# Gated attention with two heads a step on different rows of the array

## The chip, the cores and the metric

One program on one core of a Trainium2 chip. The metric is the device time of one execution in microseconds; the kernel before was run three times, median 1127.7 us (1127.27 to 1127.97).

## What is computed

Four layers in a row, each added to its input and normalised: linear attention, gated attention, decay attention, and grouped attention with experts. The change touches the second alone. On 4 sequences of 256 tokens and width 256 (x comes reshaped as such), with 16 heads of 16 columns:

```python
gating = softmax(x @ W_gate.T); idx = argmax(gating)
indicator = one_hot(idx, H); gating_top1 = indicator * max(gating)
q, k, v = split(x @ W_qkv.T)
k_shared = einsum('bth,bthd->btd', indicator, k)
v_shared = einsum('bth,bthd->btd', gating_top1, v)
att = einsum('bhqd,bkd->bhqk', q, k_shared) / sqrt(16)
att = softmax(where(causal, att, -inf))
y = einsum('bhqk,bkd->bhqd', att, v_shared)
```

Each token picks the key and value of one head, so all 16 heads of a sequence share one set of 16-wide keys and values; only the queries differ.

## The kernel before

`layer0_gated_attention` is one block, with a program for each engine. Instructions of an engine run in the order written; engines wait for each other by semaphores. The 1024 tokens are 8 tiles of 128. PSUM has 8 banks of 512 fp32 columns.

*Entry.* The programs of the loop are written once and run twice (`Fori`, two sequences each), so all waits are raised by a constant lead: each engine first raises its semaphores by 8 (`give_lead`, L92; TensorE nine of them, L790, VectorE ten, ScalarE six).

*Gate and projections.* TensorE multiplies the gate logits (L793), turns them (L799), and computes the queries (L802); VectorE finds the top head (L690 to L702). Then for each tile TensorE makes keys and values of all heads (L808) in one of three banks, and VectorE picks: two multiplications with the one-hot (L707, L708), a reduction over heads for the values (L710) and one for the keys (L711), and two copies (L715) that put the 16-wide key into four groups of 32 columns of `k_pad`, once at the even and once at the odd half of each group.

*Keys in eight versions.* TensorE turns `k_pad` (L818). The turned keys are copied into `k_rows` (L771 ScalarE, L722 VectorE): eight versions, each with the key in the 16 partitions of one head and zeros elsewhere, so that a product over all 128 partitions gives one head's scores. POOL clears `k_rows` and `k_pad` (L670 to L674). TensorE fills waits with products on zeros (`keep_warm`, L129: 20, 8 and, in each half of the loop, 8).

*The loop* takes one head a step, 32 in each of its two halves; VectorE first copies q and v of two sequences (L728, L729). A head has 384 columns of scores: its first 128 queries see 128 keys, the later 128 see 256. By step n, TensorE writes the mask of -1e30 into bank n % 3 as a bf16 product (L832) and adds the scores (L833: 128 columns, L834: 256); VectorE takes both maxima (L734, L735); ScalarE takes two exponentials, each with its own maximum as bias (L779); TensorE turns three 128 x 128 blocks into bank 3 or 4 (L840); VectorE copies them out (L740); for four heads together TensorE multiplies by the values on four column groups (L850, L852) into bank 6 or 7. The value tile carries a column of ones, which gives the row sums. ScalarE copies the outputs (L786), TensorE turns them back (L860), VectorE divides and adds the residual (L747, L749, L752).

TensorE's order in a step is scores(n), turn(n-2), and values every fourth step. VectorE's order is maxima(n), copy(n-3), and the outputs at fixed steps.

*Layer 0's linear attention* (`layer0_linear_attention`) has products that use 32 rows: for four heads at once, L397 (256 columns) and L399 (128 columns), each head on its own 32 partitions and bank; L235 multiplies them by the mask over two banks.

The next block, `normalise`, starts on a barrier of all engines.

## Time and profile before

| | us |
|---|---|
| median of 3 runs | 1127.7 |
| the profiled execution | 1128.49 |
| its span (first to last instruction) | 1126.6 |
| gated stage in it | 113.6 to 262.1 |

Busy shares of the span: TensorE 88%, its weight loads 71%, VectorE 65%, ScalarE 43%, POOL 34%. The mean granted TensorE clock is 0.958 of 2.4 GHz. A busy share is a mean over all stages; what one stage costs is read from the stage itself. Starts and lengths are given for single instructions or for merged runs of them ("x8"). Instructions of an engine overlap in the records, so what one costs its engine is the distance between starts, and not the length shown.

### The profile page before, as it was taken

Reading aid. Unit: us, or ns where it says so; the run is one execution under the profiler, and the core shown is the slowest. Engines: PE = TensorE matmul, PEld = TensorE weight load, DVE = VectorE, ACT = ScalarE, POOL = GpSimd, SP = SyncE. Lnnn points to the kernel's source line nnn. Section 1 sums busy time; section 2 is a strip of 40 time slices with the busy share of each in tenths; the row PEclk is TensorE's granted clock in tenths of the full one; section 3 lists DMA queues with packets and bytes.
Section 4 is the critical chain, followed back from the end, with each engine's and each line's share of the span. In section 5 each row is a group of like instructions: output and inputs, shape, how many; then the busy total and the mean of one; then the engine's idle time right before and its main releaser. Section 6 shows DMA issues by size and latency. Waiting matters only on the chain. (4 is left out here: it accounts for less than half of the span.)

```text
span 1126.6 us, 20312 instructions
## 1 busy us (share of the span) xinstructions
PE 993.5 (88%) x7119; PEld 802.2 (71%) x7119; DVE 729.7 (65%) x1456; ACT 484.3 (43%) x1076; POOL 387.3 (34%) x417
## 2 busy tenths in 40 slices
PE   9788989897999999999998889898989884999980
PEld 5455666664788888788885678686868632999970
DVE  3476677677455555565555588787878751888855
ACT  4222344444444554555444333343434331666630
POOL 2000600001576766676661244444444314000005
PEclk9899999998999999999999999999999986999995
DMA  4000100003333343233420100000100057655513
GB/s 167 1 2 1 29 1 1 1 0 121 99 98 109 96 118 109 82 115 105 118 85 6 42 21 24 19 23 0 42 0 19 1 189 247 240 214 212 198 38 112
DMA packets 55928, 87.35 MB, mean 78 GB/s; under 512 B 4784, under 2 KB 46000, under 8 KB 53680
## 3 DMA queue, kind: packets, MB, share of 16 engines
q1 hardware_dynamic: 54320, 82.19, 22.5%
q0 software_dynamic: 1536, 4.20, 1.1%
q8 instruction: 46, 0.75, 0.3%
q14 instruction: 26, 0.21, 0.1%
HBM read 75.36 MB, written 11.01 MB: 77 GB/s over the span
## 5 line engine op out<-in xcount | busy, mean ns | idle before, releaser
L1519 ACT ACTIVATE e_probs<-ps,e_neg_max 128x128 f32<-128x128 f32 (+1 forms) x128 | 52.6, 416 | 112.7 <-DVE e_neg_max L1466 112.7
L1075 DVE TENSOR_TENSOR d_s_m<-ps,d_decay 128x768 f32<-128x768 f32 x64 | 58.3, 952 | 50.6 <-PE ps L1238 50.6
L120 PE MATMUL ps<-xTl,d_wh 128*128 128x512 f32 x192 | 80.2, 418 | 0.0
L129 PE MATMUL ps<-warm 128*128 128x512 bf16 x265 | 71.4, 431 | 9.5 <-PEq L984 2.8
L120 PE MATMUL ps<-xTh,d_wh 128*128 128x512 f32 x192 | 76.4, 398 | 0.0
L120 PE MATMUL ps<-xTh,d_wl 128*128 128x512 f32 x192 | 76.4, 398 | 0.0
L120 PE MATMUL ps<-wl_gated,f_wh 128*128 128x256 f32 x240 | 70.1, 292 | 2.8 <-DVE wl_gated L1818 2.0
L779 ACT ACTIVATE g_probs<-ps,g_neg_max 128x128 f32<-128x128 f32 (+1 forms) x128 | 46.8, 417 | 55.9 <-DVE g_neg_max L735 55.6
L120 PE MATMUL ps<-wh_gated,f_wh 128*128 128x256 f32 x240 | 68.4, 285 | 0.0
L120 PE MATMUL ps<-wh_gated,f_wl 128*128 128x256 f32 x240 | 68.3, 285 | 0.0
L1158 ACT ACTIVATE d_gated_hi<-d_gated 128x512 fp32r<-128x512 f32 x32 | 20.2, 632 | 110.6 <-DVE d_gated L1081 110.6
L129 PEld LDWEIGHTS ps<-warm 128*128 128x128 bf16 x265 | 28.1, 109 | 48.2 <-issue 27.3
L1752 POOL DMA_INDIRECT xT<-slot_outs,f_slots x8 | 7.6, 949 | 154.8 <-DMA slot_outs<-f_rows 152.7
L1416 POOL TENSOR_TENSOR e_q_T<-e_by_cos,e_by_sin 128x512 f32<-128x512 f32 x34 | 43.6, 1282 | 49.7 <-DVE e_by_sin L1444 49.7
L1813 DVE TENSOR_TENSOR f_wl<-f_stage,f_wh 128x1024 fp32r<-128x1024 f32 x45 | 54.8, 1222 | 7.0 <-ACT f_wh L1897 6.0
L1064 DVE TENSOR_TENSOR wl_gated<-d_q_T,wh_gated 128x512 fp32r<-128x512 f32 x32 | 23.7, 741 | 53.7 <-ACT wh_gated L1137 53.7
L924 POOL TENSOR_TENSOR d_wh<-d_stage,d_nought 128x512 fp32r<-128x512 f32 x32 | 44.0, 1375 | 40.5 <-PE ps L120 29.8
L1425 POOL TENSOR_TENSOR e_probs<-e_probs,e_rsum 128x128 f32<-128x128 f32 x64 | 27.7, 432 | 78.8 <-DVE e_rsum L1471 78.8
L1897 ACT ACTIVATE f_wh<-f_stage 128x1024 fp32r<-128x1024 f32 x45 | 47.2, 1052 | 10.2 <-DMA f_stage<-in_w_experts 10.2
L120 PE MATMUL ps<-xTl,e_wh 128*128 128x512 f32 x88 | 39.5, 449 | 11.9 <-DVE e_by_sin L1444 5.8
L1040 POOL MEMSET d_ones<- 128x1 f32 x1 | 0.1, 98 | 143.2 <-POOLq L488 143.2
L120 PEld LDWEIGHTS ps<-wl_gated,f_wh 128*128 128x128 f32 x240 | 46.3, 193 | 3.4 <-issue 2.4
(359 smaller groups left out, 3302.4 us busy)
## 6 DMA issues: line engine op xcount, KB each, us to landing
f_stage<-in_w_experts SPq DMA_DIRECT2D x15, 1536.0 KB, 6.5
d_decay<-in_decay SPq DMA_DIRECT2D x32, 384.0 KB, 3.7
d_stage<-in_w_decay SPq DMA_DIRECT2D x32, 256.0 KB, 3.1
d_stage<-in_w_decay SPq DMA_DIRECT2D x32, 128.5 KB, 3.5
d_stage_v<-in_w_decay SPq DMA_DIRECT2D x32, 128.0 KB, 2.3
d_stage<-in_w_decay SPq DMA_DIRECT2D x32, 128.0 KB, 2.3
slot_rows<-warm SPq DMA_DIRECT2D x1, 3840.0 KB, 12.8
slot_outs<-f_rows SPq DMA_DIRECT2D x15, 256.0 KB, 2.2
```

The costliest lines, as they stand in the source:

```text
L120: mm = pe.matmul(out, w(k), x(k), start=(n == 0), stop=(n == 3 * len(ks) - 1))
L129: pe.matmul(out, c.warm16[:, 0:P], c.warm16[:, 0:out.shape[1]], start=True, stop=True)
L779: ex = act.activation(probs[:, n % 4, cols], ps[:, n % 3, cols], ACT.Exp, bias=neg_max[:, n % 4, b:b + 1])
L924: pool.tensor_tensor(wh, qk, self.nought[:].unsqueeze(1).broadcast_to((P, KD, 2 * P)), ALU.add).then_inc(self.qk_high, 1)
L1064: dve.tensor_tensor(q_lo, q_T[:], q_hi.bitcast(F32), ALU.subtract).then_inc(qk_lo, 1)
L1075: dve.tensor_tensor(s_m[:, s % 2, 2 * b:2 * b + 2, :], ps[:, 2 + 2 * b:4 + 2 * b, 0:CAUSAL], decay[:], ALU.mult).then_inc(sm_ready, 1)
L1158: act.activation(gated_hi[:], gated[:], ACT.Copy).then_inc(out_hi, 1)
L1416: pool.tensor_tensor(dst, by_cos[:, slot, :], by_sin[:, slot, :], ALU.add).then_inc(roped, 1)
L1425: pool.tensor_tensor(probs[:, u % 4, 0:P], probs[:, u % 4, 0:P], rsum[:, u % 4, 0:1].broadcast_to((P, P)), ALU.mult).then_inc(pn_ready, 1)
L1519: act.activation(probs[:, t % 4, cols], bank[:, cols], ACT.Exp, bias=neg_max[:, t % 4, b:b + 1], accum_out=sums[:, t % 4, b:b + 1]).then_i ...
L1813: dve.tensor_tensor(wl[j % 2][:, cols], stage[j % 2][:, cols], wh[j % 2][:, cols].bitcast(F32), ALU.subtract).then_inc(w_split, 1)
L1897: act.activation(wh[j % 2][:, PARTS[part]], stage[j % 2][:, PARTS[part]], ACT.Copy).then_inc(w_high, 1)
```

## The change

The body works on two heads a step, 32 steps, written out without a loop and so without the lead.

- The keys are kept in two versions (`k_par`: even and odd half of each group of 32 partitions). A score product uses only the 32 partitions of its group; the two heads of a step lie in neighbouring groups and go to two banks. `q_T` and `v_seq` and their copies are gone, and so is the clearing of `k_rows`.
- Masks stay two products over all 128 rows a step; there are two pairs of score banks (0, 1 and 2, 3) and one pair of turned banks (4, 5).
- One VectorE instruction takes the maxima of both heads, one copies both heads' turned blocks. ScalarE still has one exponential for each head and part. Outputs gather in bank 6 alone.
- VectorE reduces keys and values of a tile in one instruction; ScalarE spreads the keys (`spread_keys`) and copies the turned keys.
- The keys of sequences 2 and 3 are turned inside the loop, at steps 3 and 5.
- The warming products ahead of the loop and in it are gone; eight stand at its end.

```diff
 
     nc, ps = c.nc, c.ps
     QKV = 3 * D
-    SLOTS = 2
-    ITEMS = SLOTS * H0
-    QUADS = ITEMS // 4
-    PAD = 32
+    ROWS = PAD = 32
+    SPREAD = P + HD0
+    PER = H0 // 2
+    STEPS = BATCH * PER
+    QUADS = STEPS // 2
+    KEPT, KEPT_T = 3, 4
...
-        picked = sb("picked", [P, 2, H0, HD0])
...
-        v_pad = sb("v_pad", [P, NT, PAD])
-        k_pad = c.scratch[:].rearrange("p t (a n) -> p t a n", a=2)
-        k_rows = sb("k_rows", [P, 8, TOK])
+        picked = sb("picked", [P, 2, 2, H0, HD0])
+        kv_tok = sb("kv_tok", [P, NT, 2, PAD])
+        k_pad = sb("k_pad", [P, NT, 2 * SPREAD])
+        k_par = sb("k_par", [P, 2, TOK])
         q_all = c.xT
-        q_T = sb("q_T", [P, SLOTS, KD, SEQ])
-        v_seq = sb("v_seq", [P, SLOTS, TPB, PAD])
-        neg_max = sb("neg_max", [P, 4, 2])
-        probs = sb("probs", [P, 4, CAUSAL])
-        probsT = sb("probsT", [P, 8, CAUSAL])
+        neg_max = sb("neg_max", [P, 4, 2, 2])
+        probs = sb("probs", [P, KEPT, 2, CAUSAL])
+        probsT = sb("probsT", [P, KEPT_T, 2, CAUSAL])
...
+        def banks(n):
+            return 2 * (n % 2)
+
+        def heads(n):
+            quad, par = n % PER // 2, n % 2
+            return [(4 * quad + par, par, 2 * (quad % 2), quad // 2), (4 * quad + par + 2, par, 2 * (quad % 2) + 1, quad // 2)]
+
+        def out_bank(b, t):
+            return ps[:, 0 if b == BATCH - 1 and t == 1 else 7, :]
...
         @block.gpsimd
         def _(pool):
-            give_lead(pool, pool_sems)
-            pool.memset(c.scratch[:], 0.0).then_inc(padded, 1)
-            pool.memset(v_pad[:], 0.0).then_inc(padded, 1)
-            pool.wait_ge(padded, LEAD + 2)
-            pool.memset(v_pad[:, :, HD0:HD0 + 1], 1.0).then_inc(padded, 1)
-            pool.memset(k_rows[:], 0.0).then_inc(padded, 1)
+            pool.memset(kv_tok[:], 0.0).then_inc(padded, 1)
+            pool.memset(k_pad[:], 0.0).then_inc(padded, 1)
+            pool.wait_ge(padded, 1)
+            pool.memset(kv_tok[:, :, 1, HD0:HD0 + 1], 1.0).then_inc(padded, 1)
             following.prepare(pool)
 
         @block.vector
         def _(dve):
-            give_lead(dve, dve_sems)
-            link = Chain(dve, chain, LEAD)
+            link = Chain(dve, chain)
...
+            dve.wait_ge(padded, 3)
+
+            def pick(t):
+                dve.wait_ge(kv_ps, t + 1)
+                kv = ps[:, 5 + t % 3, :].rearrange("p (a h d) -> p a h d", a=2, h=H0)
+                for a, hot in enumerate((one_hot, top_hot)):
+                    mul = dve.tensor_tensor(picked[:, t % 2, a], kv[:, a], hot[:, t, :].unsqueeze(2).broadcast_to((P, H0, HD0)), ALU.mult)
+                mul.then_inc(picked_ps, 1)
+
+            def gather(t):
+                dve.wait_ge(picked_ps, t + 1)
+                dve.tensor_reduce(kv_tok[:, t, :, 0:HD0], picked[:, t % 2].rearrange("p a h d -> p a d h"), X, ALU.add).then_inc(kv_ready, 1)
+
+            def maxima(n):
+                dve.wait_ge(s_ps, n + 1)
+                need(dve, p_ready, n - 3)
+                pair = ps[:, banks(n):banks(n) + 2, :]
+                dve.tensor_reduce(neg_max[:, n % 4, 0], pair[:, :, 0:P], X, ALU.max, negate=True)
+                dve.tensor_reduce(neg_max[:, n % 4, 1], pair[:, :, P:CAUSAL], X, ALU.max, negate=True).then_inc(nm_ready, 1)
+
+            def copy_turned(n):
+                dve.wait_ge(t_ps, n + 1)
+                need(dve, pv_ps, (n - KEPT_T) // 2 + 1)
+                dve.tensor_copy(probsT[:, n % KEPT_T], ps[:, 4:6, 0:CAUSAL]).then_inc(pT_ready, 1)
+
+            def outputs(b, t):
+                seq = TPB * b + t
+                turned = out_bank(b, t).rearrange("p (h r) -> p h r", h=H0)
+                dve.wait_ge(o_turned, seq + 1)
+                dve.reciprocal(rsum[:, t, :], turned[:, :, HD0]).then_inc(rs_ready, 1)
+                dve.wait_ge(rs_ready, seq + 1)
+                dve.tensor_tensor(o_tok[:, t], turned[:, :, 0:HD0], rsum[:, t, :].unsqueeze(2).broadcast_to((P, H0, HD0)), ALU.mult).then_inc(o_scaled, 1)
+                dve.wait_ge(o_scaled, seq + 1)
+                dve.tensor_tensor(c.y[:, seq, :], o_tok[:, t].rearrange("p h d -> p (h d)"), c.x[:, seq, :], ALU.add)
+
             for t in range(NT):
-                dve.wait_ge(kv_ps, LEAD + t + 1)
-                kv = ps[:, 5 + t % 3, :].rearrange("p (a h d) -> p a h d", a=2, h=H0)
-                dve.tensor_tensor(picked[:, 0], kv[:, 0], one_hot[:, t, :].unsqueeze(2).broadcast_to((P, H0, HD0)), ALU.mult)
-                dve.tensor_tensor(picked[:, 1], kv[:, 1], top_hot[:, t, :].unsqueeze(2).broadcast_to((P, H0, HD0)), ALU.mult).then_inc(picked_ps, 1)
-                dve.wait_ge(picked_ps, LEAD + t + 1)
-                dve.tensor_reduce(v_pad[:, t, 0:HD0], picked[:, 1].rearrange("p h d -> p d h"), X, ALU.add)
-                link(dve.tensor_reduce(k_tok[:, t, :], picked[:, 0].rearrange("p h d -> p d h"), X, ALU.add))
-
-                for par in range(2):
...
-            for n in range(4):
-                half, par = n // 2, n % 2
-                dve.wait_ge(kT_ps, LEAD + n + 1)
-                for g in range(2, 4) if half else ():
-                    rows = slice(32 * g, 32 * g + 32)
-                    dve.tensor_copy(k_rows[rows, 2 * g + par, half * 512:(half + 1) * 512], ps[rows, 1 + n, :]).then_inc(kT_copied, 1)
-            with dve.Fori(0, BATCH // SLOTS) as i:
-
-                dve.wait_ge(pv_ps, LEAD + QUADS * i)
-                for u in range(SLOTS):
...
-                for n in range(ITEMS + 9):
-                    if n < ITEMS:
-                        dve.wait_ge(s_ps, LEAD + ITEMS * i + n + 1)
-                        dve.wait_ge(p_ready, LEAD + ITEMS * i + n - 3)
-                        dve.tensor_reduce(neg_max[:, n % 4, 0:1], ps[:, n % 3, 0:P], X, ALU.max, negate=True)
-                        dve.tensor_reduce(neg_max[:, n % 4, 1:2], ps[:, n % 3, P:CAUSAL], X, ALU.max, negate=True).then_inc(nm_ready, 1)
...
+            for n in range(STEPS + 2):
+                if n < STEPS:
+                    maxima(n)
+                if n >= 2:
+                    copy_turned(n - 2)
+                for b in range(BATCH - 1):
+                    if n in (PER * b + 12, PER * b + 14):
+                        outputs(b, (n - PER * b - 12) // 2)
+            for t in range(TPB):
+                outputs(BATCH - 1, t)
 
         @block.scalar
         def _(act):
-            give_lead(act, act_sems)
...
-            for n in range(4):
-                half, par = n // 2, n % 2
-                act.wait_ge(kT_ps, LEAD + n + 1)
-                for g in range(2 if half else 4):
-                    rows = slice(32 * g, 32 * g + 32)
-                    act.activation(k_rows[rows, 2 * g + par, half * 512:(half + 1) * 512], ps[rows, 1 + n, :], ACT.Copy).then_inc(kT_ready, 1)
-            with act.Fori(0, BATCH // SLOTS) as i:
-                act.activation(table[:], c.iota[:, 0:1], ACT.Exp)
-                for n in range(ITEMS + 5):
-                    if n < ITEMS:
-                        act.wait_ge(nm_ready, LEAD + ITEMS * i + n + 1)
-                        act.wait_ge(t_ps, LEAD + ITEMS * i + n - 3)
-                        for b, cols in enumerate((slice(0, P), slice(P, CAUSAL))):
...
+
+            def spread_keys(t):
+                act.wait_ge(kv_ready, t + 1)
+                dst = k_pad[:, t].rearrange("p (a n) -> p a n", a=2)[:, :, 0:P].rearrange("p a (g r) -> p a g r", g=4)[:, :, :, 0:HD0]
+                for par in range(2):
+                    act.activation(dst[:, par], kv_tok[:, t, 0, 0:HD0].unsqueeze(1).broadcast_to((P, 4, HD0)), ACT.Copy).then_inc(k_ready, 1)
+
+            def turned_keys(half, par):
+                act.wait_ge(kT_ps, 2 * half + par + 1)
+                act.activation(k_par[:, par, half * 512:(half + 1) * 512], ps[:, 7 if half else 2 + par, :], ACT.Copy).then_inc(kT_ready, 1)
+
+            def exps(n):
+                need(act, t_ps, n - KEPT + 1)
+                act.wait_ge(nm_ready, n + 1)
+                for t, cols in enumerate((slice(0, P), slice(P, CAUSAL))):
+                    for i in range(2):
+                        ex = act.activation(probs[:, n % KEPT, i, cols], ps[:, banks(n) + i, cols], ACT.Exp, bias=neg_max[:, n % 4, t, i:i + 1])
+                ex.then_inc(p_ready, 1)
+
+            def copy_out(half):
+                act.wait_ge(pv_ps, 2 * half + 2)
+                need(act, o_turned, half // 2 * TPB)
+                act.activation(o_sb[:, half % 2, :], ps[:, 6, :], ACT.Copy).then_inc(o_ready, 1)
+
+            for t in range(4):
+                spread_keys(t)
+            for par in range(2):
+                turned_keys(0, par)
+            for t in range(4, NT):
+                spread_keys(t)
+            for n in range(STEPS):
+                exps(n)
+                if n in (3, 5):
+                    turned_keys(1, (n - 3) // 2)
+                if n >= 6 and (n - 6) % 4 == 0:
+                    copy_out((n - 6) // 4)
+            copy_out(2 * BATCH - 1)
 
         @block.tensor
...
+
+            def turn_keys(half, par):
+                pe.wait_ge(k_ready, 2 * 4 * (half + 1))
+                if half and par:
+                    pe.wait_ge(kT_ready, 2 * half + 1)
+                for tile in range(4):
+                    mm = pe.transpose(ps[:, 7 if half else 2 + par, tile * P:(tile + 1) * P], k_pad[:, 4 * half + tile, par * P:(par + 1) * P], c.ident)
+                mm.then_inc(kT_ps, 1)
+
+            def masks(n):
+                need(pe, p_ready, n - 1)
+                for i in range(2):
+                    pe.matmul(ps[:, banks(n) + i, 0:CAUSAL], c.ident16[:], c.neg16[:], start=True, stop=False)
+
+            def turn(n):
+                pe.wait_ge(p_ready, n + 1)
+                need(pe, pT_ready, n)
+                for i in range(2):
+                    for k in range(3):
+                        mm = pe.transpose(ps[:, 4 + i, k * P:(k + 1) * P], probs[:, n % KEPT, i, k * P:(k + 1) * P], c.ident)
+                mm.then_inc(t_ps, 1)
+
+            def scores(n):
+                at = n // PER * SEQ
+                pair = [(ps[:, banks(n) + i, :], slice(ROWS * g, ROWS * (g + 1)), par, m) for i, (_, par, g, m) in enumerate(heads(n))]
+                for bank, rows, par, m in pair:
+                    pe.matmul(bank[:, P:CAUSAL], q_all[rows, m, at + P:at + SEQ], k_par[rows, par, at:at + SEQ], start=False, stop=False)
+                for bank, rows, par, m in pair:
+                    mm = pe.matmul(bank[:, 0:P], q_all[rows, m, at:at + P], k_par[rows, par, at:at + P], start=False, stop=True)
+                mm.then_inc(s_ps, 1)
+
+            def values(quad):
+                pe.wait_ge(pT_ready, 2 * quad + 2)
+                need(pe, o_ready, quad // 2)
+                b = quad // 4
+                out = ps[:, 6, quad % 2 * SEQ:(quad % 2 + 1) * SEQ]
+                kept = [((2 * quad + q % 2) % KEPT_T, q // 2) for q in range(4)]
+                for q, (slot, i) in enumerate(kept):
+                    pe.matmul(out[PAD * q:PAD * (q + 1), :], kv_tok[:, TPB * b, 1, :], probsT[:, slot, i, 0:SEQ], start=True, stop=False)
+                for q, (slot, i) in enumerate(kept):
+                    mm = pe.matmul(out[PAD * q:PAD * (q + 1), P:SEQ], kv_tok[:, TPB * b + 1, 1, :], probsT[:, slot, i, SEQ:CAUSAL],
+                                   start=False, stop=True)
+                mm.then_inc(pv_ps, 1)
+
+            def turn_outputs(b, t):
+                pe.wait_ge(o_ready, 2 * b + 2)
+                need(pe, o_scaled, TPB * b + (0 if b == BATCH - 1 else t))
+                for j in range(4):
+                    mm = pe.transpose(out_bank(b, t)[:, j * P:(j + 1) * P], o_sb[:, j // 2, j % 2 * SEQ + t * P:j % 2 * SEQ + (t + 1) * P], c.ident)
+                mm.then_inc(o_turned, 1)
+
             for t in range(NT):
                 tok = slice(t * P, (t + 1) * P)
                 if t >= 3:
...
-                if t >= NT - 2:
-                    half = t - (NT - 2)
-                    pe.wait_ge(q_ready, LEAD + 4)
-                    if half:
-                        keep_warm(c, pe, ps[:, 0, :], 20)
-                    pe.wait_ge(k_ready, LEAD + NT * (half + 1))
+                if t == NT - 2:
+                    pe.wait_ge(q_ready, 4)
                     for par in range(2):
-                        for tile in range(4):
-                            mm = pe.transpose(ps[:, 1 + 2 * half + par, tile * P:(tile + 1) * P], k_pad[:, 4 * half + tile, par, :], c.ident)
-                        mm.then_inc(kT_ps, 1)
-            keep_warm(c, pe, ps[:, 0, :], 8)
-            pe.wait_ge(kT_ready, LEAD + 12)
-            pe.wait_ge(kT_copied, LEAD + 4)
-            pe.wait_ge(picked_ps, LEAD + NT)
-            with pe.Fori(0, BATCH // SLOTS) as i:
...
-                keep_warm(c, pe, ps[:, 2, :], 8)
-                for n in range(ITEMS + 9):
...
+                        turn_keys(0, par)
+            pe.wait_ge(kT_ready, 2)
+            for n in range(STEPS + 2):
+                if n == PER * 2:
+                    pe.wait_ge(kT_ready, 4)
+                if n < STEPS:
+                    masks(n)
+                    scores(n)
+                if n == 2:
+                    pe.wait_ge(picked_ps, NT)
+                if n >= 2:
+                    turn(n - 2)
+                if n in (3, 5):
+                    turn_keys(1, (n - 3) // 2)
+                for b in range(BATCH - 1):
+                    if n in (PER * b + 12, PER * b + 14):
+                        turn_outputs(b, (n - PER * b - 12) // 2)
+                if n >= 4 and n % 2 == 0:
+                    values((n - 4) // 2)
+            keep_warm(c, pe, ps[:, 1, :], 4)
+            values(QUADS - 1)
+            keep_warm(c, pe, ps[:, 1, :], 4)
+            for t in range(TPB):
+                turn_outputs(BATCH - 1, t)
```

## Rows read from the trace of the kernel before

**Rows 1.** Busy time by stretch: us, busy (count) of PE, PEld, DVE, ACT, POOL, clock:
```profile
66.00:72.00 6.00, 5.47 (x96) 3.29 (x88) 2.32 (x3) 1.50 (x3) 0.00 (x0) 0.80 0.01 1
72.00:78.00 6.00, 4.94 (x54) 3.74 (x49) 5.48 (x10) 0.99 (x3) 0.00 (x0) 1.00 0.01 3
...
150.00:206.00 56.00, 50.27 (x405) 36.11 (x404) 39.74 (x112) 25.33 (x69) 0.00 (x0) 1.00 0.01 1
...
257.00:263.00 6.00, 2.82 (x22) 1.55 (x15) 2.86 (x8) 1.27 (x2) 0.00 (x0) 0.72 0.00 0
```

**Rows 2.** Timeline, one period of the loop; start, length, engine, line, operation, [idle <-releaser]:
```profile
158.59 0.64 PE L850 MATMUL ps<-g_probsT,g_v_seq 128*32 128x256 f32 x8
...
161.56 0.29 DVE L734 TENSOR_REDUCE g_neg_max<-ps 128x1 f32<-128x128 f32 x1
...
161.77 0.41 DVE L735 TENSOR_REDUCE g_neg_max<-ps 128x1 f32<-128x256 f32 x1
...
162.00 0.33 PE L832 MATMUL ps<-neg,ident 128*128 128x384 bf16 x1
...
162.10 0.55 DVE L740 COPY g_probsT<-ps 128x384 f32<-128x384 f32 x1
...
162.22 0.73 ACT L779 ACTIVATE g_probs<-ps,g_neg_max 128x128 f32<-128x128 f32 x2 [0.41 <-DVE g_neg_max L735]
...
162.38 0.60 PE L834 MATMUL ps<-g_k_rows,g_q_T 128*128 x2
...
162.82 0.49 PE L840 MATMUL ps<-consts,g_probs 128*128 128x128 f32 x3
...
163.15 0.33 PE L832 MATMUL ps<-neg,ident 128*128 128x384 bf16 x1
...
164.25 0.52 PE L840 MATMUL ps<-consts,g_probs 128*128 128x128 f32 x3
...
164.70 0.64 PE L850 MATMUL ps<-g_probsT,g_v_seq 128*32 128x256 f32 x8
...
165.49 0.34 PE L832 MATMUL ps<-neg,ident 128*128 128x384 bf16 x1
```

**Rows 3.** Timeline, VectorE: one tile's picks, the last tile's copies, the first maximum:
```profile
130.42 0.42 DVE L707 TENSOR_TENSOR g_picked<-ps,g_gate 128x256 f32<-128x256 f32 x1
...
131.20 0.60 DVE L710 TENSOR_REDUCE g_v_pad<-g_picked 128x16 f32<-128x256 f32 x1
131.72 0.58 DVE L711 TENSOR_REDUCE g_k_tok<-g_picked 128x16 f32<-128x256 f32 x1
...
132.54 0.42 DVE L707 TENSOR_TENSOR g_picked<-ps,g_gate 128x256 f32<-128x256 f32 x1
...
142.89 0.29 DVE L715 COPY scratch<-g_k_tok 128x64 f32<-128x64 f32 x2
...
150.08 0.29 DVE L734 TENSOR_REDUCE g_neg_max<-ps 128x1 f32<-128x128 f32 x1 [2.18 <-PE ps L834]
```

**Rows 4.** Timeline, end of the gated stage:
```profile
256.56 0.64 PE L850 MATMUL ps<-g_probsT,g_v_seq 128*32 128x256 f32 x8 [0.76 <-DVE g_probsT L740]
...
261.64 0.42 DVE L752 TENSOR_TENSOR y<-g_o_tok,x 128x256 f32 x1 [0.17 <-DVE g_o_tok L749]
```

**Rows 5.** Timeline, start of the gated stage:
```profile
113.64 1.80 POOL L670 MEMSET scratch<- 128x2048 f32 x1 [92.62 <-POOLq L488]
...
114.96 0.40 PE L120 MATMUL ps<-xTl,wh_gated 128*16 128x512 f32 x1 [1.65 <-issue]
```

**Rows 6.** Timeline, layer 0: scores of four heads on four row groups:
```profile
79.68 0.40 PE L416 MATMUL ps<-a_s_m,a_v_all 128*16 128x128 f32 x8
...
80.01 0.71 PE L397 MATMUL ps<-a_q_par,a_k_map 32*128 32x256 f32 x8
...
80.88 0.63 PE L414 MATMUL ps<-a_s_m,a_v_all 128*16 128x256 f32 x8
81.01 0.96 DVE L235 TENSOR_TENSOR a_s_m<-ps,consts 128x768 f32<-128x768 f32 x1 [0.64 <-PE ps L399]
```

106 lines of the change are left out of this document (15 added, 91 removed).

## The prediction

> **What bounds the kernel now.** I read three views in this order: busy time by stretch, the timeline of one period of the head loop, and the timeline around its start and end. The gated stage runs from 113.6 to 262.1 us. In its loop TensorE is busy 50.3 of 56 us and VectorE 39.7, at a granted clock of 1.00 [rows 1]. Four heads take one period, from one group of value products at 158.59 to the next at 164.70: 6.11 us [rows 2]. TensorE's own work in it, start to start: a mask and the 128-column score product 0.38, the 256-column one 0.44 (so 0.22 for 128 columns and 0.16 for the mask), three transposes 0.33, that is 1.15 a head; the value products 0.79 from 164.70 to 165.49, with 0.12 to get into them (0.45 from the last transposes less 0.33). That is 4 x 1.15 + 0.91 = 5.51. The remaining 0.6 us is TensorE standing still for VectorE's copy or ScalarE's exponentials, which answer to two or three turns of the loop back. So TensorE bounds the loop, with a small stall, and the stage is serial before and after the loop: from VectorE's last key copies at 142.89 to its first maximum at 150.08 no head is worked on, and from the last value products at 256.56 to the end of the last addition, 261.64 + 0.42 = 262.06, it is serial again, 5.5 us [rows 3, 4].
>
> **The change, part by part.**
>
> *Entry.* The block begins with POOL at 113.64, but TensorE's first product comes at 114.96: it first raises nine semaphores by the lead [rows 5]. The change drops the lead. The 1.3 us should go, as nothing else holds that product; the gate's chain, the products and the picks behind it all hang on TensorE and move up with it. Bounds: 0 to 1.3; I take 1.3.
>
> *Picks.* VectorE spends 2.12 us a tile (130.42 to 132.54): two multiplications 0.78, a reduction that starts the next 0.52 later, another, and two small copies [rows 3]. After, the two reductions are one of 512 elements and the copies go to ScalarE, which is idle there. The one reduction costs between 0.52 + 128 x 2 x 0.94 ns = 0.76 (the slope of the maxima, 0.21 for 128 and 0.33 for 256 elements [rows 2]) and twice 0.52 = 1.04; I take 0.95, nearer the top, because these strided reductions are already slower (0.60 busy) than the maxima of the same size (0.41). A tile is then 1.73, and eight save 3.1 us (2.4 to 4.6).
>
> *From the picks to the first maximum.* Now the second half of the keys is turned, copied in eighths, q and v are copied, and TensorE warms, 142.89 + 0.29 to 150.08: 6.9 us. After, the first half of the keys is turned between tiles 6 and 7, its two ScalarE copies are done while VectorE works on tiles 5 to 7, and steps 0 and 1 have their scores waiting. The second half comes at steps 3 and 5, eleven steps ahead of its first use; its two copies lie in ScalarE's slack (below). All 6.9 us go. What is late next is VectorE's tile work itself. First maximum: 150.08 - 1.3 - 3.1 - 6.9 = 138.8.
>
> *A step of the loop (two heads).* Row groups are priced by layer 0, which works four heads on four row groups [rows 6]. There 256 columns, then 128, for all four heads take 80.01 to 80.88 = 0.87, way out of the mode included, where one head here takes 0.66. VectorE sees the scores 1.00 after their start. Two heads do not go faster than four, so I take 0.87 and 1.00. The way in is 0.11 (the products at 79.68 stream 0.22, the next start 0.33 later). Masks stay at 2 x 0.16 = 0.33, transposes at 6 x 0.11 = 0.66, values at 0.91 for every second step. TensorE per two steps: 2 x (0.33 + 0.11 + 0.87 + 0.66) + 0.91 = 4.85, against 5.51.
> The Trainium skill ("TensorEngine Tiling (Array Packing)", Key Properties) says that a change of tiling mode drains the array, and every step now changes mode twice more. The trace agrees with a size: 0.11 us a change. The 64 added changes are 7 us, all in the sum above; were none paid, the saving would be 7 us more.
> VectorE: the two maxima over two banks are 0.91 by the slope (0.33 + 0.58) and 1.08 as twice the single ones; I take 0.96. The copy of 768 elements is 0.95 busy, as the layer 0 operation of that size shows (0.96), and 0.12 more until TensorE moves. ScalarE still has four exponentials, since each head has its own maximum: two take 0.73 now, so at most 1.46 to the last one's end, 2.9 of two steps, and an output copy every fourth step.
> The chain that repeats over two steps: scores of the odd step until VectorE starts 0.11 + 1.00; its maxima 0.96; then, because VectorE's order puts it there, the copy of the step two back 1.07; the transposes that wait for that copy's bank (there is one pair of turned banks now, not two alternating) 0.66; values 0.91; masks 0.33. Sum 5.04 us for four heads, above TensorE's 4.85 and far above VectorE's 2 x 1.9 and ScalarE's some 3.2. So the bound moves from TensorE's stream to a PE-DVE loop, and each four heads gain 1.07 us. Bounds: 4.8 (no mode cost on the chain) to 5.35 (the DVE operations at their upper bounds 1.08 and 1.2).
>
> *Outputs.* Six times inside the loop four transposes (0.11 each, 0.45) come into TensorE's chain: 2.7 us. VectorE's three operations for each fit beside it.
>
> *The sum of the loop.* From the first maximum to the 32nd step's: 15.5 x 5.04 + 2.7 = 80.8. Behind it, from the last maxima: maxima 0.96, then copy, turn, copy, turn, copy of the last two steps (1.07, 0.86, 1.07, 0.86, 1.07, where 0.86 is the transposes and 0.2 until they are seen), and from the last values on today's 5.5 less 0.5, since the second tile's transposes no longer wait for the first one's output: 10.9. Today's loop also drains and refills once in its middle (8 periods are 48.9 of the 56.0 us of each half, 150.08 to 262.06 halved); that goes with the unrolling and is in these figures. The end is at 138.8 + 80.8 + 10.9 = 230.5.
>
> *Clock.* TensorE has nothing to do between the scores of step 1 (about 137.5) and the first exponentials (about 141.3), where the kernel before fills such gaps with warming products. In 257 to 263 us a gap of that kind took the granted clock to 0.72, that is, partly at 1.2 GHz [rows 1]. I add 1.5 us (0 to 4) for a few periods with slow products. End: 232.0, 30.0 us earlier than 262.06. Later stages start on the barrier of this one and keep their lengths.
>
> Against the profiled execution: span 1126.6 - 30.0 = 1096.6, with the 1.9 us that lie around it 1098.5. That execution is 0.8 us above the median of the runs (1128.49 against 1127.7), so the forecast is 1097.7.
>
> **The rivals.**
>
> *The two heads do not overlap.* Layer 0 has four row groups in flight, not two, with pairs of products in another order. If two run one after the other, scores cost 1.32 + 0.22, TensorE needs 2 x 2.53 + 0.91 = 5.97 for two steps, and the loop loses 0.93 x 15.5 = 14.4: 1112. Against it speaks the same row: 4 heads in 0.87 can't come from serial products (4 x 0.66). Chance 0.08.
>
> *The clock oscillates lightly.* TensorE will idle some 0.2 us in each two steps, and its scores will fill 64 of the 128 rows. Layer 0's head loop shows both: 0.80 in 66 to 72 us, after a stretch with TensorE half idle, and 1.00 in 72 to 78 with TensorE busy 4.9 of 6 us [rows 1]. A few falls in the loop, two or three periods at 1.2 GHz, cost 4.6 each (next rival): about 1109. Chance 0.07.
>
> *The clock stays low, and the kernel is slower.* At 1.2 GHz every product doubles, and TensorE needs 9.7 us for two steps against the chain's 5.04: 4.6 more. It eats the whole 30 us from 6.5 of the 16 periods on; over the whole loop it costs 72: 1170. The masks at full height, the transposes and the values fill most of each step, as they do now at a clock of 1.00, which speaks against it; the lost warming products and the wait at the start speak for it. The Trainium skill ("TensorE: Matmul & The Clock Gate", Part 4) says that transposes do not count as activity for the clock. By that rule a third of the loop's TensorE work counts for nothing; but in the trace transposes already are 1.3 of each 6.11 us at a clock of 1.00, so I leave its weight at this chance. Chance 0.05.
>
> *VectorE's two-bank operations save nothing.* This is the upper bound above, 5.35 a period: 1102.5. It lies inside the forecast's own range.
>
> **How the numbers follow.** The forecast, 1097.7, has 0.80. Its own range is 1091 to 1105: below, no mode cost on the chain and no clock loss (15.5 x 0.24 + 1.5 + 1.5 at the picks); above, the upper DVE costs (4.8) and 2.5 of clock. The range of 8 in 10 reaches to the light clock case: 1090 to 1109. A measurement of this kernel tells some 0.2% (2.3 us) from no change. Faster: 0.80 + 0.08 + 0.07 = 0.95, less 0.01 for a loss in between; within 0.2%: 0.01; slower 0.05.
>
> **What the profile after would show.** Entry: TensorE's first product less than 0.2 us behind POOL's first memset. Picks: eight tiles at about 1.73. First maximum 11.3 us earlier. Loop: groups of value products 5.0 us apart (5.5 with output transposes between), products of two heads starting within 0.1 us of each other, the transposes released by VectorE's copy, clock 1.00 but for a dip near 141. End of the gated stage at about 232. The forecast is wrong if those groups are over 5.6 apart (serial heads, or the clock below 1), or if ScalarE's exponentials turn out to be what releases the transposes.

## The result and the profile after

| | before | after |
|---|---|---|
| median of the runs (4 each) | 1127.49 | 1097.62 (1096.07 to 1098.38) |
| the profiled execution, its span | 1128.49, 1126.6 | 1096.07, 1094.3 |
| mean granted clock | 0.958 | 0.955 |
| POOL's first memset of the block to the first maximum | 36.44 | 24.69 |
| that memset to the end of the last addition (below: the stage) | 148.42 | 118.57 |

All times are in us. After over before is 0.9734, with a 95% interval of 0.9722 to 0.9747: 29.9 us faster. The forecast was 1097.7 in a range of 1090 to 1109, so size and sign came out. The stage is 29.85 us shorter, which is all of it by the medians. The spans of the two profiled executions differ by 32.3. Of the rest, 0.7 lies in the block behind the stage (below) and 1.9 in the experts' stage. About half of the 1.9 is that, of the 16 indirect DMA issues of POOL there, two took 1.9 to 2.0 us instead of 0.96 in before and one in after; the change doesn't touch them. Outside the stage the kernels of this study differ by some 4 us (from the last addition to the end of the span: 860.9 to 865.2 us). So causes are read below from the stage of one traced execution each, and the gain of a whole kernel from its timed ratio.

The timeline of after, from the start of the block over the picks to its end (start, length, engine, line, operation, output and input, idle before it and its releaser). It is the counterpart of [rows 3, 5]:

```profile
113.70 0.53 POOL L678 MEMSET g_kv_tok<- 128x512 f32 x1 [92.86 <-POOLq L488]
113.74 0.39 PE L120 MATMUL ps<-xTl,wh_gated 128*16 128x512 f32 x1 [0.30 <-PEq L488]
...
128.05 0.74 DVE L715 TENSOR_TENSOR g_picked<-ps,g_gate 128x256 f32<-128x256 f32 x2
128.83 1.04 DVE L720 TENSOR_REDUCE g_kv_tok<-g_picked 128x32 f32<-128x512 f32 x1
129.78 0.74 DVE L715 TENSOR_TENSOR g_picked<-ps,g_gate 128x256 f32<-128x256 f32 x2
...
138.39 0.41 DVE L726 TENSOR_REDUCE g_neg_max<-ps 128x2 f32<-128x256 f32 x1
140.85 0.82 PE L833 MATMUL ps<-neg,ident 128*128 128x384 bf16 x2 [3.34 <-ACT g_probs L784]
...
221.79 0.42 DVE L726 TENSOR_REDUCE g_neg_max<-ps 128x2 f32<-128x256 f32 x1 [0.47 <-PE ps L849]
...
231.85 0.42 DVE L742 TENSOR_TENSOR y<-g_o_tok,x 128x256 f32<-128x256 f32 x1
```

The first product is 0.04 us behind the memset (1.32 before), a tile of picks takes 1.73 (2.12 before), and the first maximum stands at 138.39. Then TensorE waits 3.34 us for the first exponentials, ahead of the masks of step 2.

The loop of after, one period (TensorE, VectorE and one exponential of ScalarE, the same columns), the counterpart of [rows 2]:

```profile
187.88 0.64 PE L859 MATMUL ps<-g_probsT,g_kv_tok 128*32 128x256 f32 x8
...
188.66 0.50 PE L833 MATMUL ps<-neg,ident 128*128 128x384 bf16 x2
189.09 0.70 PE L847 MATMUL ps<-g_k_par,xT 32*128 32x256 f32 x4
...
189.63 0.39 PE L849 MATMUL ps<-g_k_par,xT 32*128 32x128 f32 x4
189.95 0.88 PE L840 MATMUL ps<-consts,g_probs 128*128 128x128 f32 x6
190.06 0.42 DVE L726 TENSOR_REDUCE g_neg_max<-ps 128x2 f32<-128x256 f32 x1 [1.12 <-PE ps L849]
190.40 0.68 DVE L727 TENSOR_REDUCE g_neg_max<-ps 128x2 f32<-128x512 f32 x1
190.66 0.49 PE L833 MATMUL ps<-neg,ident 128*128 128x384 bf16 x2
191.00 0.95 DVE L732 COPY g_probsT<-ps 128x768 f32<-128x768 f32 x1
...
191.18 1.36 ACT L784 ACTIVATE g_probs<-ps,g_neg_max 128x128 f32<-128x128 f32 x4 [1.17 <-DVE g_neg_max L727]
...
192.10 0.85 PE L840 MATMUL ps<-consts,g_probs 128*128 128x128 f32 x6
192.78 0.60 PE L869 MATMUL ps<-consts,g_o_sb 128*128 128x128 f32 x4
...
193.31 0.64 PE L859 MATMUL ps<-g_probsT,g_kv_tok 128*32 128x256 f32 x8
```

Follow the starts: values 187.88, masks 188.66, scores 189.09, maxima 190.06, copy 191.00, transposes 192.10, and 0.78 later the next values if no output transposes (L869) stand between (here they do). That is 0.78 + 0.43 + 0.97 + 0.94 + 1.10 + 0.78 = 5.00 us, and the periods measure 5.00, 5.00, 5.43, 5.44 in turn. From start to start, the 256-column products of both heads take 0.54 and the 128-column ones 0.31 to 0.32 to the transposes: 0.85 for two heads, where the forecast took 0.87 and one head before took 0.66. ScalarE's exponentials end at 192.54, behind the transposes of 192.10 that use an earlier step's, and release nothing here.

Busy time of after by stretch (us, busy and count of PE, PEld, DVE, ACT, POOL, then the granted clock, as in [rows 1]):

```profile
137.00:141.00 4.00, 0.66 (x9) 0.43 (x6) 3.30 (x7) 2.17 (x10) 0.00 (x0) 0.89 0.00 0
141.00:146.00 5.00, 5.00 (x22) 3.22 (x22) 1.98 (x3) 2.40 (x8) 0.00 (x0) 0.50 0.00 0
146.00:152.00 6.00, 6.00 (x42) 4.57 (x42) 2.95 (x6) 1.84 (x5) 0.00 (x0) 0.64 0.01 3
152.00:160.00 8.00, 8.00 (x86) 5.59 (x78) 5.49 (x10) 5.04 (x14) 0.00 (x0) 1.00 0.00 1
...
186.00:226.00 40.00, 37.68 (x375) 26.20 (x375) 32.43 (x57) 22.30 (x64) 0.00 (x0) 1.00 0.01 1
```

The wait of 3.34 us is followed by 10.2 us at 0.50, 1.2 GHz, from 140.1 to 150.3: the shares 0.89, 0.50 and 0.64 of the first three rows stand for 0.9, 5.0 and 4.3 us at the low level. From 141 to 146 there are 22 products, where the loop at 2.4 GHz gets 375 records into 40 us, 47 into 5. From 152 on the clock is 1.00.

### The profile page after: what moved, and what is told of

Read it like the earlier page. It is cut to its first block and busy times, and to the rows that moved or that the text cites. A ratio compares the mean times of both kernels' runs of the same rounds, so it can differ in the third digit from the quotient of the medians.

```text
span 1094.3 us, 19650 instructions
## 1 busy us (share of the span) xinstructions
PE 968.1 (88%) x7073; PEld 784.4 (72%) x7083; DVE 713.4 (65%) x1324; ACT 478.8 (44%) x1082; POOL 381.1 (35%) x416
## 5 line engine op out<-in xcount | busy, mean ns | idle before, releaser
L129 PE MATMUL ps<-warm 128*128 128x512 bf16 x221 | 59.4, 427 | 9.8 <-PEq L1364 3.2
L784 ACT ACTIVATE g_probs<-ps,g_neg_max 128x256 f32<-128x256 f32 (+1 forms) x128 | 43.3, 423 | 37.7 <-DVE g_neg_max L727 37.7
L129 PEld LDWEIGHTS ps<-warm 128*128 128x128 bf16 x229 | 24.2, 108 | 41.3 <-issue 22.8
L963 POOL TENSOR_TENSOR d_wh<-d_stage,d_nought 128x256 fp32r<-128x256 f32 x32 | 26.9, 841 | 64.2 <-PE ps L120 64.2
## 6 DMA issues: line engine op xcount, KB each, us to landing
slot_rows<-warm SPq DMA_DIRECT2D x1, 3840.0 KB, 12.8
```

The lines of the kernel that those rows point to most:

```text
L129: pe.matmul(out, c.warm16[:, 0:P], c.warm16[:, 0:out.shape[1]], start=True, stop=True)
L784: ex = act.activation(probs[:, n % KEPT, i, cols], ps[:, banks(n) + i, cols], ACT.Exp, bias=neg_max[:, n % 4, t, i:i + 1])
L963: pool.tensor_tensor(wh, g, self.nought[:].unsqueeze(1).broadcast_to((P, KD, P)), ALU.add).then_inc(self.g_high, 1)
```

## The experiments

My theory: the loop's period is a chain through TensorE and VectorE; the two heads overlap because their products use different rows; and the gain has four sources, the entry, the picks, the keys turned early, and a shorter loop without a drain in its middle. Rivals: the heads on different rows don't matter; TensorE's stream alone bounds; two-bank operations carry the gain; the clock stays low for longer than I allowed. Every edit is to the kernel after, unless it says before.

| kernel | first maximum | stage | four heads | clock low for | timed median | ratio to before (95%) |
|---|---|---|---|---|---|---|
| same_rows | 24.73 | 145.85 | 6.15 | 30.7 | 1122.71 | 0.9942 (0.992 to 0.9965) |
| same_rows_warm | 24.74 | 132.86 | 6.15 | 0 | 1112.90 | 0.9862 (0.9846 to 0.9878) |
| no_masks | 24.70 | 113.37 | 4.56 | 13.7 | 1090.37 | 0.9680 (0.9645 to 0.9716) |
| single_banks | 24.72 | 120.91 | 5.19 | 10.2 | 1098.97 | 0.9747 (0.9723 to 0.9772) |
| after | 24.69 | 118.57 | 5.00 | 10.2 | 1097.62 | 0.9734 (0.9722 to 0.9747) |
| warm_start | 24.72 | 114.34 | 5.00 | 0 | 1091.10 | 0.9675 (0.9659 to 0.9692) |
| values_later | 24.72 | 115.12 | 4.76 | 10.2 | 1090.99 | 0.9674 (0.9656 to 0.9693) |
| late_warm | 24.73 | 110.67 | 4.76 | 0 | 1089.75 | 0.9657 (0.9635 to 0.9679) |
| keys_first | 31.37 | 130.17 | 5.00 | 30.7 | 1106.74 | 0.9818 (0.979 to 0.9846) |
| four_slots (before) | 36.19 | 143.13 | 6.1 to 7.2 | 0 | 1120.61 | 0.9946 (0.9926 to 0.9965) |
| with_lead | 26.05 | 121.79 | 5.00 | 13.7 | 1100.23 | one run |
| no_end_warm | 24.73 | 118.81 | 5.00 | 10.2 | 1096.64 | one run |
| before_no_warm (before) | 36.39 | 151.97 | 6.1 to 7.3 | 13.7 | 1134.55 | one run |

First maximum and stage count from POOL's first memset of the block. "Four heads" is the commonest distance between groups of value products; before measures 6.11 to 7.34. The fifth column is how long the granted clock stood at 0.50 around the start of the loop, by its mean in stretches around both edges. A difference of two stages contains that of their clocks. The column of the period doesn't, nor does that of the first maximum, but for keys_first and before_no_warm.

### same_rows: the two heads share their rows

```diff
-            quad, par = n % PER // 2, n % 2
-            return [(4 * quad + par, par, 2 * (quad % 2), quad // 2), (4 * quad + par + 2, par, 2 * (quad % 2) + 1, quad // 2)]
+            quad, s = n % PER // 2, n % 2
+            return [(4 * quad + 2 * s + par, par, 2 * (quad % 2) + s, quad // 2) for par in range(2)]
...
-                kept = [((2 * quad + q % 2) % KEPT_T, q // 2) for q in range(4)]
+                kept = [((2 * quad + q // 2) % KEPT_T, q % 2) for q in range(4)]
```

> The changed kernel, but with the two heads of a step taken from the even and odd half of ONE group of 32 rows, so that their score products share rows and can't overlap. All else, the result included, is the same. Theory (the row groups carry the loop's gain): the scores of a step last 1.41 us instead of 0.87, TensorE needs 2 x (0.33 + 0.11 + 1.41 + 0.66) + 0.91 = 5.93 us for four heads and becomes the bound again; the groups of value products lie 5.9 apart instead of 5.00, and the kernel is 14 to 15 us slower than the changed one, near 1112. Rival (the gain comes from elsewhere, from the front and the unrolling, and the overlap is worth little): at most 2 us slower.

The products of a step now take 0.97 + 0.53 = 1.50 us (196.26 to 197.23 to 197.76, the transposes, in the trace of same_rows_warm) against 0.85 (1.41 expected). The period is 6.15, close to the 6.11 of the kernel before: what the change gains in a period goes with the shared rows. But the stage lost 27.3, half as much again as the loop explains, and the clock shows where. Busy time of same_rows by stretch:

```profile
152.00:160.00 8.00, 8.00 (x37) 5.03 (x36) 1.98 (x3) 1.84 (x5) 0.00 (x0) 0.50 0.01 3
160.00:170.00 10.00, 10.00 (x45) 7.51 (x47) 3.85 (x6) 3.04 (x9) 0.00 (x0) 0.50 0.00 0
170.00:180.00 10.00, 10.00 (x79) 7.04 (x72) 5.17 (x10) 3.64 (x11) 0.00 (x0) 0.97 0.01 2
```

The low clock lasts to 170.6 us here, so this run mixes two causes, which the next section parts. Its ten timed executions scatter from 1114.97 to 1125.72. The two fastest, 1114.97 and 1115.09, have the highest mean clock, 0.953 against 0.944 to 0.951. So the low clock probably differs in length between executions of one kernel; only one of them was traced, at 1122.49.

### warm_start and same_rows_warm: the wait at the start filled

```diff
+                if n == 2:
+                    keep_warm(c, pe, ps[:, 4, :], 14)
```

These warming products stand ahead of the masks of step 2, and go to a bank that nothing uses yet.

> The changed kernel with 14 warming products between the scores of step 1 and the masks of step 2, where TensorE stands still for 3.3 us; the granted clock is 0.50 to 0.78 from 140 to 152 us behind that gap. Theory (the fall of the clock is caused by the gap and costs a few slow periods): the clock stays at 1.00 and the gated stage ends 2 to 3 us earlier (its time from the first maximum to the end was 93.9 us against 91.7 worked out without a fall). Rival (the steps near the start wait for VectorE and ScalarE anyway): under 0.5 us.

> The edits of same_rows and warm_start together, to part the two costs that same_rows mixed: its stage is 27.3 us longer than the changed kernel's, with periods of 6.15 instead of 5.00, and its granted clock stays at 0.50 from the gap to about 170 us. Theory (the serial products cost 1.15 a period, the rest is the clock's long fall, which the gap starts): with the gap filled the clock stays at 1.00, the periods stay 6.15, and the stage is 15.5 x 1.15 = 18 us longer than warm_start's 114.3, at 132. Rival (scores of few rows hold the clock down by themselves): the clock falls again, and the stage stays above 138.

The busy time by stretch of warm_start:

```profile
137.00:141.00 4.00, 3.62 (x21) 1.70 (x20) 3.47 (x7) 2.17 (x9) 0.00 (x0) 1.00 0.00 0
141.00:146.00 5.00, 4.88 (x40) 3.54 (x40) 3.49 (x6) 3.05 (x10) 0.00 (x0) 1.00 0.01 3
146.00:152.00 6.00, 6.00 (x61) 4.43 (x60) 4.06 (x7) 3.77 (x12) 0.00 (x0) 1.00 0.00 1
```

The clock stays at 1.00, 40 products instead of 22 fit into 141 to 146 us, and the stage is 118.57 - 114.34 = 4.23 shorter, more than the 2 to 3 expected: this is the price of the low clock in after. Timed, the kernel gains 6.5 by the medians. The 2.3 beyond the stage are within the scatter of the rest named above, and no run shows their cause. same_rows_warm has no low clock either, and against warm_start its stage is 18.5 longer, 21.8 timed. That is 16 periods by 1.15. Overlap of the heads is thus worth 18.5 us of the stage. Without the warming products same_rows is 13.0 longer than same_rows_warm: this is the price of its low clock.

### no_masks: is the period the chain or TensorE's stream?

```diff
-                for i in range(2):
-                    pe.matmul(ps[:, banks(n) + i, 0:CAUSAL], c.ident16[:], c.neg16[:], start=True, stop=False)
```

The first score product of each bank starts it instead. This leaves out the causal mask.

> The changed kernel without the mask products (the causal mask is left out of the scores); the score products start their banks instead of adding to them. Theory (a loop of TensorE and VectorE bounds the steps, in which the masks stand once in two steps): the period falls from 5.00 by one step's masks, 0.33, to 4.67, and the kernel by 15.5 x 0.33 = 5 us. Rival (TensorE's own stream bounds it, 4.84 of 5.00): both steps' masks go, 0.66 to 0.7, the period falls to 4.3 to 4.35 and the kernel by 10 us.

Two masks and the entry into the products on 32 rows take 0.43 a step, 0.86 of TensorE's stream in a period. The period fell by 0.44, from 5.00 to 4.56, which is one step's, as the chain passes masks once in two steps. A period bound by TensorE's stream alone would have fallen by the whole 0.86. The stage fell by 5.2 and not by 16 x 0.44 = 7.0. Its clock was low for longer, 13.7 us at the start instead of 10.2 and 3.4 more at the end of the loop (216.7 to 220.1 us), which goes in the right direction; no run prices it by itself. TensorE's own stream in a period is 4.84 (from starts: values 0.78, then 0.43 + 0.54 + 0.31 for each of two steps, transposes 0.71 ahead of masks and 0.78 ahead of values), 0.16 under the chain.

### values_later and late_warm: the value products taken out of the chain

```diff
+                if n >= 5 and n % 2:
+                    values((n - 5) // 2)
                 if n >= 2:
                     turn(n - 2)
...
-                if n >= 4 and n % 2 == 0:
-                    values((n - 4) // 2)
```

Output transposes and additions go to steps 13 and 15 of a sequence, the copies to a step later. late_warm has this edit and the 14 products of warm_start.

> The changed kernel with the value products moved one step later, ahead of the transposes, and the output copies and transposes one step later with them. Theory (the values lie in the PE-DVE loop behind the transposes that wait for the copy): the loop of the odd steps now has 0.97 + 0.94 + 1.10 + 0.78 + 0.43 = 4.2 us, TensorE's stream of 4.84 becomes the bound, and the stage ends 15.5 x 0.16 = 2.5 us earlier. Rival (the stall only moves to another step, as the banks of the turned blocks are still one pair): no change, period 5.00.

> The edits of warm_start and values_later together. Theory: both gains add up, 4.5 to 5.5 us faster than the changed kernel, near 1092.5. Rival: only one of them is left.

The value products now start straight behind a step's scores, when VectorE is at that step's maxima. Timeline of values_later, with the value products (L859) between scores and transposes:

```profile
199.96 0.64 PE L859 MATMUL ps<-g_probsT,g_kv_tok 128*32 128x256 f32 x8
...
204.83 0.39 PE L849 MATMUL ps<-g_k_par,xT 32*128 32x128 f32 x4
205.15 0.64 PE L859 MATMUL ps<-g_probsT,g_kv_tok 128*32 128x256 f32 x8
...
205.94 0.87 PE L840 MATMUL ps<-consts,g_probs 128*128 128x128 f32 x6
206.65 0.49 PE L833 MATMUL ps<-neg,ident 128*128 128x384 bf16 x2
```

The period is 4.76, or 5.19 with output transposes, as here. TensorE's wait of 0.16 is gone, and 0.07 of the stream with it: transposes run into masks in 0.71 where they ran into value products in 0.78. The stage is 3.45 shorter (2.5 expected) with the clock still low for 10.2 us, and 7.9 shorter in late_warm (4.5 to 5.5 expected), so by the stage the two gains add up. Timed they don't: the medians of warm_start, values_later and late_warm are 6.5, 6.6 and 7.9 below that of after, and their intervals overlap. late_warm has the shortest stage and the lowest median of the study, 0.9657 of before and by the two ratios 0.992 of after; that it beats the other two is shown for the stage alone.

### single_banks: maxima and copies bank by bank

```diff
-                dve.tensor_reduce(neg_max[:, n % 4, 0], pair[:, :, 0:P], X, ALU.max, negate=True)
-                dve.tensor_reduce(neg_max[:, n % 4, 1], pair[:, :, P:CAUSAL], X, ALU.max, negate=True).then_inc(nm_ready, 1)
+                for t, cols in enumerate((slice(0, P), slice(P, CAUSAL))):
+                    for i in range(2):
+                        last = dve.tensor_reduce(neg_max[:, n % 4, t, i:i + 1], pair[:, i, cols], X, ALU.max, negate=True)
+                last.then_inc(nm_ready, 1)
```

The copy of the turned blocks is cut in two in the same way.

> The changed kernel with VectorE's two-bank operations taken apart again: four maxima and two copies a step instead of two and one. Theory (VectorE stands in the chain of a period only once with its maxima and once with its copy): maxima 0.21 + 0.21 + 0.33 + 0.33 = 1.08 instead of 0.94, copy 0.47 + 0.55 + 0.12 instead of 1.10; the period goes from 5.00 to 5.2, the kernel 3 us slower. Rival (the two-bank operations are a main part of the gain): VectorE per two steps goes from 3.6 to 4.0 us plus the waits for each, and the kernel is 8 us or more slower.

A period is 0.19 longer, from 5.00 to 5.19 (5.2 expected), and the stage 2.3. The timed intervals of single_banks and after overlap, so of the whole kernel the run can't tell a loss. The two-bank operations carry little of the gain.

### four_slots: the kernel before without the seam

```diff
-    SLOTS = 2
+    SLOTS = 4
```

> The kernel before, with its loop over heads written for all four sequences in one pass instead of two passes of two. Nothing else of the change. Theory: of the 112.0 us from the first to the last head, 2 x 8 periods of 6.11 are 97.8; one of the two drains and refills of 7.1 goes, less 0.9 for copying q and v of two more sequences ahead: 6 us faster than the kernel before, near 1121.5. Rival (the seam between the halves costs nothing, since the later half would be held by the same engines anyway): no change. Second rival (written out twice as long, the instruction stream is fetched too slowly): slower.

The loop of before runs through four sequences in one pass. The stage is 5.3 shorter, 4.5 of it between the first and the last maximum, and the kernel is 0.9946 of before (0.9926 to 0.9965). So the drain and refill in the middle cost some 5, and unrolling alone brings them back.

### keys_first: the second half of the keys turned ahead of the loop

```diff
-                if n in (3, 5):
-                    turn_keys(1, (n - 3) // 2)
...
+            for par in range(2):
+                turn_keys(1, par)
+            pe.wait_ge(kT_ready, 4)
```

ScalarE's `turned_keys(1, ...)` moves ahead of its loop likewise.

> The changed kernel with the second half of the keys turned and copied ahead of the first scores again, not at steps 3 and 5. Theory: the first scores wait for the keys of tile 7 (VectorE's last reduction ends at 138.4), their spreading 0.4, the transposes 0.5 and two copies of 0.6: the first maximum comes at about 142 instead of 138.4, 3.5 us later, while steps 3 and 5 lose 0.5 to 1 each of TensorE and ScalarE time: 2 to 3 us slower in all. Rival (the start is bounded by VectorE's tiles, and the keys are hidden anyway): no change.

The timeline of keys_first from the last pick on:

```profile
138.07 1.08 PE L827 MATMUL ps<-consts,g_k_pad 128*128 128x128 f32 x4 [3.94 <-ACT g_k_pad L773]
139.19 0.60 ACT L777 ACTIVATE g_k_par<-ps 128x512 f32<-128x512 f32 x1 [1.18 <-PE ps L827]
139.93 1.09 PE L827 MATMUL ps<-consts,g_k_pad 128*128 128x128 f32 x4 [0.78 <-ACT g_k_par L777]
...
141.71 0.82 PE L833 MATMUL ps<-neg,ident 128*128 128x384 bf16 x2 [0.69 <-ACT g_k_par L777]
142.46 1.22 PE L847 MATMUL ps<-g_k_par,xT 32*128 32x256 f32 x4
...
144.16 0.42 DVE L726 TENSOR_REDUCE g_neg_max<-ps 128x2 f32<-128x256 f32 x1 [6.58 <-PE ps L849]
```

Turn, copy, turn, copy, masks and scores stand in a row, as in before, and VectorE waits 6.58 us. The first maximum is 6.7 later, not 3.5. The wait comes so early that the chain itself runs at the low clock: from the first mask to the maximum 2.45 us, in after's loop 0.43 + 0.97 = 1.40, and from one key turn to the next 1.86. Two more rows show how long the low clock lasts, to 168.9 us, with TensorE busy in every microsecond of them:

```profile
152.00:160.00 8.00, 8.00 (x46) 4.82 (x43) 3.96 (x6) 2.71 (x8) 0.00 (x0) 0.50 0.01 3
160.00:170.00 10.00, 10.00 (x59) 6.55 (x59) 4.05 (x7) 3.31 (x9) 0.00 (x0) 0.56 0.00 0
```

The stage loses 11.6, timed 9.1. Turning the keys inside the loop thus saves 6.7 at the first maximum, some of it clock already. The other 4.9 of the stage are put down to the longer low clock by difference; a run of keys_first with its waits filled, which would show it, is missing.

### with_lead, no_end_warm, before_no_warm

with_lead lets TensorE raise a spare semaphore nine times at its entry, as before did; no_end_warm drops the eight products at the end of after's loop; before_no_warm drops before's 20, 8 and 8.

```diff
+            give_lead(pe, [idle_sem] * 9)
...
-            keep_warm(c, pe, ps[:, 1, :], 4)
             values(QUADS - 1)
-            keep_warm(c, pe, ps[:, 1, :], 4)
```

> The changed kernel with nine raises of an unused semaphore at the start of TensorE's program, as the lead of the kernel before had them. Theory (the lead's raises cost TensorE 1.3 us): the first product comes 1.3 us behind POOL's first memset instead of 0.04, and the first maximum 1.3 us later from there, 26.0 instead of 24.7. Rival (the entry's delay was the loop's set-up or the larger number of semaphores): unchanged.

> The changed kernel without the eight warming products at the end of the stage. The next block took 11.3 us from its first statistics to the barrier behind it, and 12.0 in the kernel before, whose warming products ran at a lowered clock there. Theory (the end's warming products hold the clock over the seam): without them the clock falls near the end, the output transposes or the next block's products are slow, and stage and block together are 0.7 to 1.5 us longer. Rival: unchanged, as the products of the next block warm the engine in time.

> The kernel before without its own warming products ahead of the loop and at the start of each half (20, 8 and 8 twice). Theory (a gap ahead of the loop lowers the clock, and it takes many periods to come back): the granted clock falls to 0.50 at about 140 us and stays there for 9 us or more; the stage of 148.4 us becomes 4 us or more longer. Rival (the loop of the kernel before uses all 128 rows and keeps the clock up by itself): the fall is short, under 1.5 us.

The entry of with_lead in its timeline:

```profile
112.25 0.53 POOL L678 MEMSET g_kv_tok<- 128x512 f32 x1 [90.95 <-POOLq L488]
...
113.64 0.39 PE L120 MATMUL ps<-xTl,wh_gated 128*16 128x512 f32 x1 [1.65 <-issue]
```

The first product is 1.39 behind the memset, and the first maximum 1.36 later than in after: nothing hides the lead. The stage is 3.2 longer. The other 1.9 come with a low clock of 13.7 us instead of 10.2. no_end_warm shows no use of the products that it drops: from the last step's maxima to the end of the stage it takes 10.45, after 10.48. Its normalise block (statistics to the next barrier) takes 11.65 instead of 11.30, but warm_start, values_later, late_warm, keys_first and no_masks, which all have the products, take 11.71. before_no_warm shows the low clock in the other kernel: with TensorE idle for 5.93 us from 139 on, the clock is at 0.50 from 142.2 to 155.8 and again for 6.8 us at the seam (0.90 over 190 to 225 us). The stage is 3.55 longer, a little under the 4 expected.

## Why the prediction was right

*Entry and front: right.* 1.3 taken, 1.36 measured by with_lead. Picks 1.73 a tile as forecast; the one reduction starts the next operation after 0.95, as taken. The first maximum was put at 138.8 and came at 138.39, 11.75 us earlier from the memset (11.3 forecast); keys_first, 6.7 later, shows that where the second half of the keys is turned carries over half of it.

*Two heads on different rows: right, and the largest single part.* 0.87 and 1.00 were read from layer 0's four heads [rows 6]; 0.85 and 0.97 were measured. same_rows_warm measures what the rival "the heads do not overlap" described: that rival said 1112 and the kernel takes 1112.9, although with two differences that partly cancel: its period is 6.15 and not 5.97, and its clock doesn't fall. What [rows 6] couldn't say, and experiments did, is what two groups of rows cost: 0.85, hardly less than four, and little more than half of the 1.50 that the two heads take on shared rows.

*The PE-DVE loop as the bound: right.* The period was forecast at 5.04 and measures 5.00, TensorE's stream at 4.85 and measures 4.84. no_masks took one step's masks from the period and not two; values_later took the value products out of the chain and left the period at the stream. The upper bound for VectorE, 5.35, was too high: its own terms give 5.04 + 0.12 + 0.13 = 5.29, and even with single operations the period is 5.19. The Trainium skill ("TensorEngine Tiling (Array Packing)", Key Properties) warned of a drain at each change of mode; in this trace masks to scores are 0.43 where the masks alone are 0.33, so 0.10 to 0.11 a change, the size already in the sum.

*The sum of the loop: too high by 1.7.* From the first maximum to the 32nd step's I had 80.8 without a loss of clock. warm_start, which has none, measures 217.71 - 138.56 = 79.15. The term that was too large is 15.5 x 5.04. At 5.00 it is 0.6 less. And the first two steps have no copy and no values in the chain yet: the third step's maximum comes 3.85 behind the first (138.56 to 142.41), where 5.04 was counted, 1.2 less. The tail behind it was 10.9 and is 231.85 + 0.42 - 221.79 = 10.48.

*The clock: the mechanism right, its size too low.* The gap was put at 137.5 to 141.3 and lies at 137.5 to 140.85. I took 1.5 us for the fall, with a bound of 4; it costs 4.23, outside even that bound. By the prediction's own price (4.66 lost in 9.7 us at 1.2 GHz) 1.5 us stand for 3.1 us of low clock, where the 10.2 us that came would have been priced at 4.9. The error is in how [rows 1] was read: 0.72 over 257 to 263 us is 3.4 us of low clock, but the row ends in the middle of the fall. Two stretches of before show the whole of that fall and an earlier one in layer 0, as long as that of after:

```profile
44.60:54.80 10.20, 6.33 (x74) 4.04 (x72) 5.47 (x6) 0.00 (x0) 0.00 (x0) 0.50 0.01 2
259.60:266.40 6.80, 5.15 (x14) 2.21 (x15) 5.23 (x22) 1.49 (x2) 0.00 (x0) 0.50 0.43 146
```

This error and those of the three terms above (0.4 + 1.7 + 0.4) cancel: the end was forecast at 232.0 and came at 232.27. That a forecast right to 0.1 us rested on an error of 2.7 and errors of 2.5 in the other direction is luck.

*The rivals that did not come.* In the loop the clock is 1.00 from 152 to 226 us, with TensorE waiting 0.16 a period and its scores on 64 of 128 rows. So neither the light nor the lasting fall came. The Trainium skill ("TensorE: Matmul & The Clock Gate", Part 4) says that a transpose doesn't count as busy for the clock in the same way as other products. Here 1.3 to 1.8 us of each 5.0 to 5.4 are transposes (27 to 33%; the prediction's "a third" is the upper end), and once the clock is at 1.00 it stays there. Whether they lengthen the low clock at the start no run tests. same_rows and keys_first come near to a longer loss: 13 and about 5 us in one block.

*Not foreseen:* the normalise block behind the stage is 0.7 us shorter (statistics to the next barrier 12.02 in before, 11.30 in after), with its first warming products in 4.48 us instead of 6.47: in before they run partly at 0.50 (the stretch to 266.4 above), in after at 1.00. This isn't the work of the warming products at the end of the loop, as far as the runs show: warm_start, values_later, late_warm, keys_first and no_masks have them as well, and there the clock is at 0.50 from 0.5 to 1.6 us behind the end of the stage on, and the block's products take 6.16.

Where the 29.85 of the stage come from: 1.4 entry (with_lead), 3.1 picks (eight tiles by 0.39), 7.3 keys and warming ahead of the loop (what remains of the 11.75 to the first maximum), 5.3 the seam (four_slots). The rest, 12.8, is the loop itself net of the 4.2 that the clock takes back. 16 periods by 1.1 would be 17.6, and 17.6 - 4.2 = 13.4 agrees to 0.6. Parts that come from runs of other kernels than after need not add up exactly.

## What to carry to other kernels

Price products on parts of the rows by the same form elsewhere in the trace, then look for the cycle that repeats over the program order of two engines: it, and not the busier engine, can set the period, and moving one step of the order (here the value products ahead of the transposes) then shortens it. Where a change removes warming products or opens a wait of TensorE ahead of a loop (2.07 to 5.93 us here), look up in the trace how long the clock stayed low after earlier waits, over stretches that hold the whole fall, and price that length (10 to 31 us here). Then fill the wait: here it cost nothing, as TensorE had nothing else to do. When a forecast comes out, check its terms one by one, since two errors may have met.
